# Group averages in three products: channels laid out as c = 3p + k in an attention and convolution kernel

## What is computed

```
x = x + attention(_gn(x))     # 1x1 projections q, k, v; 2D rotary; elu + 1; linear attention, 6 heads; 1x1 projection
x = x + convolution(_gn(x))   # 1x1; 8x8 patch FFT filter; 3x3 depthwise; gelu gate; 1x1

def _gn(v, G=32, eps=1e-5):
    g = v.reshape(B_, G, C_ // G, H_, W_)
    m = jnp.mean(g, axis=(2, 3, 4), keepdims=True)
    s = jnp.var(g, axis=(2, 3, 4), keepdims=True)
    return ((g - m) / jnp.sqrt(s + eps)).reshape(v.shape)
```

## Time and profile before

| | us |
|---|---|
| median of 3 runs | 3602.86 |
| the runs | 3592.69 to 3609.84 |
| the profiled execution, its own time | 3610.5 |
| its span in the trace | 3608.4 |
| PE busy | 3351.8 (93%) |
| DVE busy | 3006.7 (83%) |
| ACT busy | 1709.3 (47%) |
| POOL busy | 2046.6 (57%) |

### The profile page before, as it was taken

The page is one execution under the profiler, slowest core; times in us unless marked ns, Lnnn a source line. Parts: engine busy times, 40 slices in busy tenths (PEclk is TensorE's granted clock), DMA queues, the critical chain, the costliest instruction groups (busy, mean ns, idle before and its releaser), DMA issues. The chain is left out here.

```text
span 3608.4 us, 50305 instructions
## 1 busy us (share of the span) xinstructions
PE 3351.8 (93%) x17430; PEld 2901.3 (80%) x17430; DVE 3006.7 (83%) x5252; ACT 1709.3 (47%) x3138; POOL 2046.6 (57%) x1343
## 2 busy tenths in 40 slices
PE   5999989999899999999999999999999999999998
PEld 4987779777797777977789777897778967799776
DVE  7977988779897698987989869788798887988877
ACT  1433844338443474434744357342574426644265
POOL 2554755547556474564755647456474565654555
PEclk9999999999999999999999999999999999999999
DMA  6214332143312333123321233312332133321422
GB/s 220 71 45 158 115 105 72 61 149 108 119 63 67 135 120 108 62 79 123 132 97 62 97 115 124 104 62 100 120 123 97 53 123 105 123 90 60 140 97 96
DMA packets 185339, 369.89 MB, mean 103 GB/s; under 512 B 7770, under 2 KB 8834, under 8 KB 184834
## 3 DMA queue, kind: packets, MB, share of 16 engines
q1 hardware_dynamic: 185090, 366.68, 29.7%
HBM read 265.99 MB, written 100.66 MB: 102 GB/s over the span
## 5 line engine op out<-in xcount | busy, mean ns | idle before, releaser
L1124 PE MATMUL bank<-w_hi,x_hi 128*128 128x384 f32 x2304 | 803.1, 349 | 19.3 <-ACT vt L575 10.0
L444 POOL TENSOR_TENSOR t<-t 128x768 f32<-128x768 f32 x256 | 534.8, 2089 | 468.8 <-DVE t L829 464.8
L1125 PE MATMUL bank<-w_lo,x_hi 128*128 128x384 f32 x2304 | 778.8, 338 | 0.0
L993 DVE SCALAR_TENSOR_TENSOR bank<-big,wdw,bank 128x512 f32<-128x512 f32 x1072 | 750.5, 747 | 22.4 <-PE bank L1305 19.4
L437 POOL TENSOR_TENSOR x_lo<-xa,x_hi 128x512 fp32r<-128x512 f32 x360 | 459.0, 1290 | 526.0 <-ACT x_hi L564 526.0
L509 POOL TENSOR_TENSOR prod<-prod 128x512 f32<-128x512 f32 x320 | 412.2, 1288 | 256.5 <-ACT prod L667 238.1
L1129 PE MATMUL bank<-w_hi,x_lo 128*128 128x384 f32 x2304 | 531.5, 339 | 0.5 <-POOL x_lo L437 0.5
L569 ACT ACTIVATE t<-t 128x384 f32<-128x384 f32 x256 | 134.7, 526 | 767.5 <-POOL t L444 749.9
L1124 PEld LDWEIGHTS bank<-w_hi,x_hi 128*128 128x128 f32 x2304 | 434.1, 188 | 26.4 <-issue 25.8
L1125 PEld LDWEIGHTS bank<-w_lo,x_hi 128*128 128x128 f32 x2304 | 434.9, 189 | 2.3 <-issue 1.7
L1129 PEld LDWEIGHTS bank<-w_hi,x_lo 128*128 128x128 f32 x2304 | 413.4, 188 | 1.4 <-POOL x_lo L437 1.4
(11 more groups left out here) (131 smaller groups left out, 7042.9 us busy)
## 6 DMA issues: line engine op xcount, KB each, us to landing
xr<-x SPq DMA_DIRECT2D x128, 768.0 KB, 4.8
xa<-x SPq DMA_DIRECT2D x64, 768.0 KB, 6.3
x_scratch<-xr SPq DMA_DIRECT2D x64, 768.0 KB, 3.3
xa<-x_scratch SPq DMA_DIRECT2D x64, 768.0 KB, 6.0
xr<-x_scratch SPq DMA_DIRECT2D x64, 768.0 KB, 4.9
out<-xr SPq DMA_DIRECT2D x64, 768.0 KB, 3.3
big<-x SPq DMA_DIRECT2D x8, 768.0 KB, 10.2
w_raw<-wqkv_t SPq DMA_DIRECT2D x1, 1728.0 KB, 7.0
```

The costliest lines, as they stand in the source:

```text
L444: nc.gpsimd.tensor_tensor(a, a, b[:, :, ::-1, :], ALU.add).then_inc(s_add, 1)
L993: nc.vector.scalar_tensor_tensor(dst, src, wdw[:, k, q:q + 1], so_far, ALU.mult, ALU.add)\
L1124: nc.tensor.matmul(dst, hi(k), whi(k), start=(k == 0), stop=False)
L1125: nc.tensor.matmul(dst, hi(k), wlo(k), start=False, stop=False)
```

## The change

Channel c now lies in partition p = c // 3, block k = c % 3. The tensors x, scratch and out are read and written by that rule, and so are the rows of the first weights; the columns of the output weights and the biases are permuted on the host to match. Twelve neighbouring channels are then four neighbouring partitions in all three blocks, so one 128 x 128 matrix averages all: three products into the same two columns, where there were seven. The small tiles behind it shrink from 128 x 6 to 128 x 2, as all three blocks share a group's mean and factor.

In the last chunk of part b, block 0 goes by ACT (bias, from bank 5) and POOL (residual) instead of DVE; DVE's order is residual 1, statistics 0, statistics 1, residual 2, statistics 2. And DVE reads the key sums of L932 from PSUM bank 0 instead of `kbc`.

```diff
-    x_v = x.rearrange("b (k p) (c n) -> b p k c n", p=P, n=CHUNK)
+    x_v = x.rearrange("b (p k) (c n) -> b p k c n", p=P, n=CHUNK)
 (out_v, x1_v, wqkv_t and w_in_t in the same way)
-        t_gavg = sb("t_gavg", [P, len(GBLOCKS), P])
+        t_gavg = sb("t_gavg", [P, P])
@@ group_avg, PE
-                    for m in range(KB):
-                        ks = [k for k, mm in GBLOCKS if mm == m]
-                        for k in ks:
-                            ins = nc.tensor.matmul(bank[7][:, 2 * m:2 * m + 2], t_gavg[:, GBLOCKS.index((k, m)), :], src(k),
-                                                   start=(k == ks[0]), stop=(k == ks[-1]))
+                    for k in range(KB):
+                        ins = nc.tensor.matmul(bank[7][:, 0:2], t_gavg[:, :], src(k), start=(k == 0), stop=(k == KB - 1))
@@ group_norm, DVE (L788 to L795 all go from [:, :, :] of 128 x 6 to [:, :] of 128 x 2)
-                pm = bank[7][:, 0:2 * KB].rearrange("p (m s) -> p s m", s=2)
-                nc.vector.tensor_copy(gmean[:, :, :], pm)
-                nxt(nc.vector.tensor_tensor(dev[:, :, :], mv[:, :, :, 0], pm, ALU.subtract), 2)
+                pm = bank[7][:, 0:2]
+                nc.vector.tensor_copy(gmean[:, :], pm)
+                nxt(nc.vector.tensor_tensor(dev[:, :, :], mv[:, :, :, 0], pm.unsqueeze(2).to_broadcast([P, 2, KB]),
+                                            ALU.subtract), 2)
@@ after part b, POOL
+                gp.wait_ge(s_xr[1], (i * 12 + 8) * 16)
+                gp.wait_ge(s_proj, i * NCH + NCH)
+                nc.gpsimd.tensor_tensor(xr[:, 1, 0], xr[:, 1, 0], proj[:, :], ALU.add).then_inc(s_sum, 1)
@@ after part b, ACT
+                act.wait_ge(s_out, (i * 16 + NCH) * 3 + 4)
+                act.wait_ge(s_sum, i * NCH + NCH - 1)
+                nc.scalar.activation(proj[:, :], bank[5][:, :], ACT.Identity, bias=bfc_c[:, 0:1]).then_inc(s_proj, 1)
@@ last chunk of part b, DVE
-                        for m in range(KB):
-                            residual(i * 16 + c - 1, i * 12 + 4 + h + par, 1 - par, True, blocks=(m,))
-                            dve.wait_ge(s_res, r + (m + 4))
-                            ins = nc.vector.bn_stats(bn_x1[:, m, c - 1, :], xr[:, 1 - par, m])
-                        ins.then_inc(s_x1s, 1)
+                        residual(i * 16 + c - 1, i * 12 + 4 + h + par, 1 - par, True, blocks=(1,), inc=2)
+                        dve.wait_ge(s_sum, i * NCH + NCH)
+                        nc.vector.bn_stats(bn_x1[:, 0, c - 1, :], xr[:, 1 - par, 0])
+                        dve.wait_ge(s_res, r + 5)
+                        nc.vector.bn_stats(bn_x1[:, 1, c - 1, :], xr[:, 1 - par, 1])
+                        residual(i * 16 + c - 1, i * 12 + 4 + h + par, 1 - par, True, blocks=(2,))
+                        dve.wait_ge(s_res, r + 6)
+                        nc.vector.bn_stats(bn_x1[:, 2, c - 1, :], xr[:, 1 - par, 2]).then_inc(s_x1s, 1)
@@ middle piece, DVE
-                                        kbc[:, :].unsqueeze(1).to_broadcast([P, TPC - TG, C]), ALU.mult).then_inc(s_kd, 1)
+                                        bank[0][:, 0:C].unsqueeze(1).to_broadcast([P, TPC - TG, C]), ALU.mult).then_inc(s_kd, 1)
```

More of the change, by code:

```diff
@@ L39 @@
 THETA = 10000.0
-GBLOCKS = [(k, m) for m in range(KB) for k in range(KB) if abs(k - m) <= 1]
 def rotary_tables():
@@ L100, in constants @@
     phi, sel = patch_basis()
-    g = np.kron(np.eye(C // GROUP), np.full((GROUP, GROUP), 1.0 / GROUP)).astype(np.float32)
-    gavg = np.stack([g[k * P:(k + 1) * P, m * P:(m + 1) * P] for k, m in GBLOCKS], axis=1)
+    gavg = np.kron(np.eye(C // GROUP), np.full((GROUP // KB, GROUP // KB), 1.0 / GROUP)).astype(np.float32)
     return {
@@ L377, in part_b @@
                         wait(s_res, (i * 16 + c) * 3 + 3)
[L378 to L379 removed]
+                        wait(s_sum, i * NCH + c - 1)
                         sp.dma_start(chunk_of(x1_v, i, c - 2), xr[:, par]).then_inc(s_st[par], 16)
@@ L553, in normalise @@
                 for k in range(KB):
-                    nc.scalar.activation(xa[:, par, k], xa[:, par, k], ACT.Identity, bias=shift[:, 1, k:k + 1],
-                                         scale=rstd[:, 1, k:k + 1]).then_inc(s_nrm, 1)
+                    nc.scalar.activation(xa[:, par, k], xa[:, par, k], ACT.Identity, bias=shift[:, 1:2],
+                                         scale=rstd[:, 1:2]).then_inc(s_nrm, 1)
             def high_part(m, par, patches=False):
@@ L581, in group_root @@
                 act.wait_ge(s_gs, f * 11 + 5)
-                nc.scalar.activation(gstd[:, :, :], gvar[:, :, :], ACT.Sqrt).then_inc(s_ga, 1)
+                nc.scalar.activation(gstd[:, :], gvar[:, :], ACT.Sqrt).then_inc(s_ga, 1)
             group_root(0)
@@ L795, in group_norm @@
-                nxt(nc.vector.scalar_tensor_tensor(shift[:, :, :], gmean[:, :, :], -1.0, rstd[:, :, :], ALU.mult, ALU.mult), 11)
+                nxt(nc.vector.reciprocal(rstd[:, :], gstd[:, :]), 6)
+                nxt(nc.vector.tensor_tensor(newt[:, :], rstd[:, :], rstd[:, :], ALU.mult), 7)
+                nxt(nc.vector.tensor_tensor(newt[:, :], newt[:, :], gvar[:, :], ALU.mult), 8)
+                nxt(nc.vector.tensor_scalar(newt[:, :], newt[:, :], -0.5, 1.5, ALU.mult, ALU.add), 9)
+                nxt(nc.vector.tensor_tensor(rstd[:, :], rstd[:, :], newt[:, :], ALU.mult), 10)
@@ L915, in low_q, with residual @@
                                                 ALU.subtract).then_inc(s_ql, 1)
-                def residual(r, loads, par, bias, blocks=(0, 1, 2)):
+                def residual(r, loads, par, bias, blocks=(0, 1, 2), inc=1):
                     dve.wait_ge(s_xr[par], loads * 16)
@@ L927, in residual @@
                             ins = nc.vector.tensor_tensor(xr[:, par, m], ps, xr[:, par, m], ALU.add)
-                        ins.then_inc(s_res, KB - m if m == blocks[-1] and len(blocks) > 1 else 1)
+                        ins.then_inc(s_res, KB - m if m == blocks[-1] and len(blocks) > 1 else inc)
                 dve.wait_ge(s_ka, i * 5 + 1)
```

54 lines of the change are left out of this document (25 added, 29 removed).

## The result

The changed kernel takes 3593.28 us (median; 3585.18 to 3602.68), the kernel before takes 3605.87 (3592.69 to 3612.18). The ratio is 0.9967, 95% interval 0.9958 to 0.9976: 12.6 us faster. The forecast was 3570 us, 33 us faster, in a range of 3553 to 3590. The time lies above that range. Faster was right, its size was not.

What follows compares the result with a forecast made beforehand. PE and DVE alternate over most of an image, but one dependent chain bounds each norm. Norm products 29.6, start's norm 3.4, smaller operations there 0.2 and `t_gavg` load 0.4 sum to 33.6 us: 3602.86 to 3570, range 3553 to 3590.

Steps and rivals of the forecast that it cites:

- The products: Norm of each image: averages cut from 14 PE records to 6, stretch 12.88 to 9.2 us, 29.6 us less for eight.
- L788 to the first L1124: Norm's piece after the second average, up to the convolution's first product: 3.66 us in the last image, taken as 3.2.
- from the first product to the second average: Norm's piece from the first average's first product to the second's: 4.96 us in the last image, taken as 3.1, PE-bound.
- L779 to the first product: Norm's opening piece, from L779 to the first product of the first average: 1.58 us, unchanged.
- The smaller operations: Eight shrunken operations in a row in each norm: 0 to 0.29 us less, taken as 0.2.
- The last chunk: Last chunk before each norm: saved 0.73 us DVE residual costed at nothing, 0.6 spent waiting for POOL; +1.6 to -4 us.
- The transfers: DMA loads under the new layout: rows stay 2 KB, only their order differs; taken as nothing, 3 us either way.
- rival D: Last chunks' loads lengthen by their new addresses, making the kernel slower; decides from 4.1 us more per load; chance 0.03.
- The factor from PSUM: DVE's L932 product with an operand in PSUM: no gain, at worst 0.1 us lost per image, 0.8 in all.
- B: Full clock returns sooner in the norm's gaps: 4.7 us less per image, 42 us, 3561 us; chance 0.13.
- C: Slow clock keeps its place and reaches the convolution: 1.7 of each 3.7 us given back, 3583 us; chance 0.22.
- E: Three products take as long as seven, or saved time becomes a wait behind the norm: 3602 to 3590 us; chance 0.10.

## Why the prediction was right or wrong

**The products** (29.6 us for eight images): right as a mechanism, and right in size where the transfers are the old ones: 3.9 us per image against 3.7. In after's profiled execution it is (103.00 - 85.00) / 8 = 2.25. Two pieces are longer there than in my sum: "L788 to the first L1124", 4.01 instead of 3.2 us, and from the first product to the second average, 3.65 instead of 3.1, as I had the first average run mostly at the full clock (0.83 us), and five of the eight took 1.44. "L779 to the first product" is 1.58 us as assumed, but PE idles longer ahead of it. And the 0.8 us per image that are given back behind the norm stood at nothing, so that the products alone brought 27 us and not 33. The start's norm gave 3.5 us against 3.4: each of its averages went from 3.15 to 1.44 us, though the trace has no clock of 0.50 there, so the pace is shown and its cause isn't.

**The smaller operations** (0.2 us per norm): next to nothing. L791 to L814 is 1.68 us instead of 1.74. L791 at 2 columns takes 160 ns, where L788 took 164 at 6: 4 ns less and not the 36 of the slope of 9 ns a column, my estimate from 24 and 6 columns. So it came out near the bound of nothing.

**The last chunk** (nothing): right in each part. The new wait for POOL is 0.56 us (0.6 forecast), landing to the end of the last statistics is 3.97 us (4.15 forecast, 4.24 before), and the whole was worth 0 when taken out.

**The transfers** (nothing, 3 us either way): this step failed. I looked at the rows' length, which stays 2 KB, and at their order, which costs nothing that can be told (3579.15 us reversed, 3577.78 with the old views), and not at the form of the pattern in the built program. The form cost 10 to 15 us, 14 by the reversed blocks: 0.1 to 0.9 us at the last chunk and 0.9 to 1.4 at the start of part a, in each image, in the two pairs that differ in it alone. Inside the norm `xa` did come next in line where the clock stayed up, as the prediction said, with the waits above. My rival D named the place (the last chunks' loads) but priced it as a matter of addresses, and I gave it 0.03 as a case that only counts from 4.1 us per load. It had to be a term, not a case: 0.5 us on a store, 0.2 on the load behind it and 0.2 on each issue, at two places of every image where nothing covers them.

**The factor from PSUM** (nothing, 0.8 us lost at worst): failed. I priced the instruction and not its neighbour. The row that could have warned me was in the trace of before: the same product on POOL takes 2482 ns beside L932, while the 1536 columns of L468, twice as many, take 3497.

```profile
L468 POOL TENSOR_TENSOR qn<-big,kbc 128x1536 f32<-128x1536 f32 x56 | 195.8, 3497 | 0.0
...
L474 POOL TENSOR_TENSOR qn<-big,kbc 128x768 f32<-128x768 f32 x8 | 19.9, 2482 | 58.8 <-ACT kbc L604 58.8
```

Half of 3497 is 1749; the 733 ns more were the price to be gained.

**The addresses of the tiles**: in no step of mine. By the pace they cost after 4.5 us, and 22.5 us against the best address seen.

**The sum that holds.** Three products -27 (alone, in the kernel before), PSUM -5, the form of the transfers +14, the address +4.5, the last chunk 0: -13.5 us, and -12.6 were measured. Against the forecast 33 us the norm is 6 short, the form takes 14 and the address 4.5, and PSUM gives 5. The terms come from different kernels, whose profiled executions have mean granted clocks from 0.976 to 0.989; the form's lies between 10 and 15, and the factor brought 13 us in its own run. So that the sum agrees to 1 us is luck. The norm's term stands here with the old transfers; whether it is as large beside the new ones isn't shown.

**The rivals.** B (clock back sooner) came in part: three stretches of eight in the kernel with three products alone and three with the old last chunk, none in after's one profiled execution. But before with 32 and with 64 bytes more, fourteen records and all, had one and three of them, so the shorter averages aren't what decides it. C's giving back was 0.8 us per image, not 1.7. E is out: at the half clock (granted 0.50) six records take 1.44 us and less where fourteen took 2.98 to 3.15, and at the full clock (1.00) 0.83 where they took 1.72. I gave B and C each a chance for all eight images; the runs show a mixture from image to image, and with PE's gap ahead of the first average closed by six more fillers it was 22 stretches of 24 at 0.99 or 1.00 instead of 16 of 64.

## What to carry to other kernels

When a view of DRAM is changed, look at the access pattern that comes out in the built program and at the issue time of the transfer, not only at the row length: reversing the blocks' order kept all of this layout's use without the 14 us that its form cost. When a tile is added or shrunk, compare the start addresses of the hot matmul operands before and after, since an unused small tile moved the pace of 256 tiles by 1.3 to 1.6%, which was 17 to 21 us and more than the whole change brought. And price an instruction by its neighbours too: what runs longer on the engine beside it (POOL's product by 0.67 us), and how long PE idles ahead of it (with twenty fillers the granted clock was 0.99 or 1.00 in the 22 stretches with a gap under 1 us, and 0.58 and 0.63 in the two with more).

## What the runs showed of the hardware

- PE's products of `x_hi` and `x_lo` (fp32r, 128x384) run at 5.389, 5.407 or 5.319 us a tile with `x_hi` at 0, 32 or 64 modulo 128 bytes and the tiles around it moving along. Only these three were seen.
- A transfer of 384 rows of 2 KB whose DRAM side is one run of 384 rows and whose SBUF side is 128 x 3 is issued in 0.56 us, with three blocks on both sides in 0.37; its store lands after 3.7 to 3.9 us (the medians of four kernels) instead of 3.3 to 3.5 (of twelve).
- POOL's 128x768 product took 2.48 us beside a DVE product with two SBUF operands and 1.81 us beside the same product with one of them in PSUM.
- With twenty fillers ahead of an average of 2 columns, in 22 of 24 stretches PE idled under 1 us before it and the granted clock was 0.99 or 1.00; with fourteen fillers PE idled 0.98 to 3.67 us and the clock was at 1.00 in 16 of 64.
